# Wo of the last head loaded, bounded and scaled at other slots, and values stored as whole rows

## The reference, cut to what is computed

```
xn = layernorm(x)
q = xn @ Wq;  k, v = split(xn @ Wkv)
scores = q k^T / sqrt(32) + slope[head] * (s - t), only s <= t
attn = softmax(scores);  o = attn v
attention = concat(o) @ Wo + bo
gate = xn @ Wg^T;  up = xn @ Wu^T        # codes looked up and scaled by blocks of 32
ffn = (gelu_tanh(gate) * up) @ Wd^T
out = x + attention + ffn
```

## Time and profile before

| | |
|---|---|
| median of 3 runs | 1640.24 us (1639.86 to 1642.94) |
| the profiled execution | 1641.02 us |
| its span in the trace | 1639.2 us |
| busy: TensorE | 1429.3 us, 87% |
| busy: VectorE | 1297.4 us, 79% |
| busy: GpSimd | 1000.8 us, 61% |
| busy: ScalarE | 975.9 us, 60% |
| DMA share of the 16 engines, q1 | 80.8% |

### The profile page before, as it was taken

The page is one execution under the profiler, slowest core; times in us unless marked ns, Lnnn a source line. Parts: engine busy times, 40 slices in busy tenths (PEclk is TensorE's granted clock), DMA queues, the critical chain, the costliest instruction groups (busy, mean ns, idle before and its releaser), DMA issues.

```text
span 1639.2 us, 28993 instructions
## 1 busy us (share of the span) xinstructions
PE 1429.3 (87%) x9281; PEld 684.1 (42%) x9281; DVE 1297.4 (79%) x2639; ACT 975.9 (60%) x2124; POOL 1000.8 (61%) x670
## 2 busy tenths in 40 slices
PE   5978998999889989889989989899888999897598
PEld 4743443444334434444434434344433444343243
DVE  8858787888868788888868788888868788875466
ACT  3347666666656666665666666666656666664330
POOL 3226676666656677666656666777656766774341
PEclk9979999999999999999999999999999999998799
DMA  7878969788897888798889879886998988887665
GB/s 219 231 176 175 171 119 170 149 161 154 160 163 144 160 155 165 145 152 149 166 158 153 157 151 160 147 174 136 173 154 154 153 158 153 147 152 133 120 155 198
DMA packets 784799, 260.97 MB, mean 159 GB/s; under 512 B 734512, under 2 KB 755896, under 8 KB 784392
## 3 DMA queue, kind: packets, MB, share of 16 engines
q1 hardware_dynamic: 780328, 253.48, 80.8%
q10 hardware_dynamic: 4320, 5.64, 1.0%
HBM read 52.30 MB, written 21.89 MB: 45 GB/s over the span
## 4 chain that ended last, share of the span: by engine, by line
DVE 30%; PE 18%; issue 14%; ACT 10%; DMA 10%; POOL 6%; SPq 4%; ACTq 0%; DVEq 0%; POOLq 0%
DMA pt<-pair 8%; PE up_ps L1348 5%; ACT p L1475 5%; POOL pair L1734 5%; DVE mxp L1588 4%; DVE acc L1545 4%; PE gate_ps L1348 4%; PE s_ps L1370 3%; DVE dec L369 3%; DVE wf L382 3%; DVE prod L1569 2%; PE down_ps L1326 2%; ACT gl L1456 2%; DVE s_ps L1590 2%; DVE dec L373 2%
## 5 line engine op out<-in xcount | busy, mean ns | idle before, releaser
L1734 POOL TENSOR_TENSOR pair<-p,pair 128x1024 f16<-128x1024 f32 (+7 forms) x384 | 615.2, 1610 | 347.3 <-ACT pair L1485 344.9
L1475 ACT ACTIVATE p<-s_ps,shift 128x512 f32<-128x512 f32 (+3 forms) x640 | 393.2, 619 | 222.6 <-DVE shift L1609 220.9
L1370 PE MATMUL s_ps<-kst,qst 128*128 128x512 f32 (+3 forms) x640 | 344.7, 540 | 115.2 <-ACT p L1475 106.9
L1485 ACT ACTIVATE pair<-p 128x1024 f16<-128x1024 f32 (+7 forms) x384 | 308.3, 808 | 100.4 <-DMA pt<-pair 97.3
L1588 DVE TENSOR_REDUCE mxp<-s_ps 128x1 f32<-128x512 f32 x384 | 260.2, 683 | 103.5 <-PE s_ps L1370 101.5
L1742 POOL TENSOR_TENSOR il<-prod,ih 128x512 f16<-128x512 f32 x128 | 156.2, 1220 | 149.7 <-DVE ih L1577 149.7
L1370 PEld LDWEIGHTS s_ps<-kst,qst 128*128 128x128 f32 x640 | 123.2, 193 | 233.6 <-ACT p L1475 157.9
L1326 PE MATMUL down_ps<-wh,ih 128*128 128x512 f16 x506 | 195.9, 387 | 28.2 <-DVE acc L1545 28.2
L1326 PE MATMUL down_ps<-wh,il 128*128 128x512 f16 x506 | 193.0, 381 | 16.0 <-POOL il L1742 16.0
L1348 PE MATMUL up_ps<-xh,wh 128*128 128x512 f16 x512 | 200.2, 391 | 0.0
L1348 PE MATMUL gate_ps<-xh,wh 128*128 128x512 f16 x512 | 197.6, 386 | 0.6 <-DVE gl L1561 0.6
(11 more groups left out here) (249 smaller groups left out, 2064.6 us busy)
## 6 DMA issues: line engine op xcount, KB each, us to landing
o<-oraw SPq DMA_DIRECT2D x256, 64.0 KB, 2.0
qst<-q_parts SPq DMA_DIRECT2D x192, 64.0 KB
q_parts<-o SPq DMA_DIRECT2D x24, 256.0 KB, 3.4
pt<-pair SPq DMA_TRANSPOSE x384, 4.3
raw<-L_ffn_gate_W_packed_dram SPq DMA_DIRECT2D x16, 256.0 KB, 3.1
raw<-n_L_ffn_up_W_packed_dram SPq DMA_DIRECT2D x16, 256.0 KB, 3.0
raw<-L_ffn_down_W_packed_dram SPq DMA_DIRECT2D x32, 128.0 KB, 2.6
o<-l_recips SPq DMA_DIRECT2D x64, 64.0 KB, 2.1
```

The source lines that it names most:

```text
L1370: nc.tensor.matmul(s_ring[n % len(s_ring)][:, 0:cols], qst[:, c % 2, i4 * P:(i4 + 1) * P], kst[:, m * CH:m * CH + cols], start=True, stop= ...
L1475: nc.scalar.activation(p32[p % PR][:, at:at + cols], s_ring[n % len(s_ring)][:, 0:cols], ACT.Exp, bias=shift[t % len(shift)][:, 0:1], accu ...
L1485: nc.scalar.activation(pair[n % PH][:, 0:cols], p32[n % PR][:, 0:cols], ACT.Copy).then_inc(phi_done, 1)
L1734: nc.gpsimd.tensor_tensor(pair[n % PH][:, cols:2 * cols], p32[n % PR][:, 0:cols], pair[n % PH][:, 0:cols], ALU.subtract).then_inc(plo_done, 1)
```

## The change

Six slot numbers move, one step is cut in two, and the layout of the stored values changes.

- `LOAD_EARLY_AT` 12 becomes 1; `WO_MAX_AT` (17, 18, 19, 20) becomes (14, 16, 17, 19).
- `spread_tops` is divided: `store_tops` stores the maxima at slot 21; `spread_tops`, which waits for the store, reads them back and issues `load_full(sp, 1)`, is at slot 28 instead of 27.
- `WO_SCALE_AT` 29 becomes 37, `WO_HI_AT` (31, 32, 33, 34) becomes (38, 40, 42, 43), `wo_low` follows one slot behind each; `LOAD_X_AT` 41 becomes 46.
- `vt` and `v_s` hold two fields instead of four; the fills and their semaphore go; `load_v` is one DMA of 256 KB, 2 KB in a row per partition on both sides.

```diff
-LOAD_EARLY_AT, LOAD_FULL_AT, SPREAD_TOPS_AT, LOAD_X_AT = 12, 25, 27, 41
+LOAD_EARLY_AT, LOAD_FULL_AT, STORE_TOPS_AT, SPREAD_TOPS_AT, LOAD_X_AT = 1, 25, 21, 28, 46
-WO_MAX_AT, WO_SCALE_AT, WO_HI_AT = (17, 18, 19, 20), 29, (31, 32, 33, 34)
+WO_MAX_AT, WO_SCALE_AT, WO_HI_AT = (14, 16, 17, 19), 37, (38, 40, 42, 43)
-    v_s = nc.dram_tensor("v_parts", [KVH, P, NT, 4 * HD], F16, kind="Internal").ap()
+    v_s = nc.dram_tensor("v_parts", [KVH, P, NT, 2 * HD], F16, kind="Internal").ap()
-    vt = wh[1][:, 0:2].rearrange("p m a n -> p (m a n)").rearrange("p (j g a d) -> p j g a d", j=TPC, g=KVH, a=4)
+    vt = wh[1][:, 0].rearrange("p a n -> p (a n)").rearrange("p (j g a d) -> p j g a d", j=TPC, g=KVH, a=2)
-                nc.gpsimd.memset(vt[:, :, :, 1, :], 1.0).then_inc(vt_filled, 1)
-                nc.gpsimd.memset(vt[:, :, :, 3, :], 0.0).then_inc(vt_filled, 1)
-                    for part in range(2):
-                        sp.dma_start(vst[:, :, part * HD:(part + 1) * HD],
-                                     v_s[i // REP, :, :, 2 * part * HD:(2 * part + 1) * HD]).then_inc(v_in, 16)
+                    sp.dma_start(vst[:], v_s[i // REP]).then_inc(v_in, 16)
+                            if s == STORE_TOPS_AT:
+                                store_tops()
-                def spread_tops():
+                def store_tops():
                     sp.wait_ge(wtop_done, 1)
                     sp.dma_start(w_s.rearrange("(p o) -> p o", o=1), wtop).then_inc(wtop_out, 16)
+
+                def spread_tops():
                     sp.wait_ge(wtop_out, 16)
-                            pe.wait_ge(v_in, (h // REP + 1) * 32)
+                            pe.wait_ge(v_in, (h // REP + 1) * 16)
```

More of the change, by code:

```diff
@@ L539, in preamble @@
         vscale_done = sem("vscale_done")
-        vt_filled = sem("vt_filled")
         os_turned = sem("os_turned")
@@ L572, in store_v @@
                     sp.wait_ge(v_lo, c + 1)
-                    if c == 0:
-                        sp.wait_ge(vt_filled, 2)
                     store_values(sp, c)
@@ L921, in values_lo @@
                     nc.vector.scalar_tensor_tensor(
-                        vt[:, :, :, 2, :].rearrange("p j g d -> p (j g) d"), vps[:].rearrange("p (n d) -> p n d", d=HD),
+                        vt[:, :, :, 1, :].rearrange("p j g d -> p (j g) d"), vps[:].rearrange("p (n d) -> p n d", d=HD),
                         vscale[:, 0:1], vt[:, :, :, 0, :].rearrange("p j g d -> p (j g) d"), ALU.mult, ALU.subtract
```

## The result

The changed kernel took **1612.92 us** (median of 4 runs, 1609.45 to 1614.90), the kernel before 1640.05 us beside it (4 runs): ratio 0.9837, 95% interval 0.9822 to 0.9852. Forecast were 1606 us, with a range of 1594 to 1618. So it is faster by 27 us where 35 were forecast. The profiled execution took 1613.71 us, its span is 1611.9 us.

What follows compares the result with a forecast made beforehand. TensorE was taken to set the pace in the running stream, with losses waiting for Wo, the stored maxima and the values. Gains of 19 + 2 + 12 + 2 = 35 us off 1641.02 gave 1606 us, range 1594 to 1618.

Steps and rivals of the forecast that it cites:

- Term 1: Last head, wait for the stored maxima: storing at slot 21, reading at 28, using at 37 gains 19 us (14 to 21).
- rival (a): Last head: transposes held behind the store at slot 21, 5 us of idle and 2 of clock, 1613 us; chance 0.15.
- transposes over 8 us behind the store: Store at slot 21: transposes taking over 8 us behind it would show the prediction wrong.
- 1.8 us given back at the end: Before the last values product: moved weight splittings let the last transpose start earlier, 1.8 of TensorE's 2.75 us saved.
- Term 2: Last head, wait for Wo: its load moved from slot 12 to slot 1 gains 2 us (-4 to +14).
- rival (b): Slot 1 has room: transposes pass the Wo load and values wait nowhere, gain 14, 1594 us; chance 0.08.
- (c): Hold at slot 1 felt twice, at tiles 5 and 7 and again at the scores: -4, 1612 us; chance 0.15.
- Term 3: Three values loads at group boundaries: one DMA of whole rows, shorter waits and no clock fall, 12 us (4 to 16).
- 4 us as a sign of being wrong: Values loads: one landing after 4 us or more would show the prediction wrong.
- Term 4: First values load, ahead of the loop: a saved second issue and a lighter queue gain 2 us (0 to 5).
- Rival (e): Single values DMA falls on one engine at 25 GB/s: 14 us slower, 1654 us; chance 0.03.
- Rival (d): Values load gains only its issue time, 1.0 us each, and the clock still falls: 1614 us; chance 0.13.

Runs made afterwards that it cites:

- low_moved: The changed kernel with the splitting of Wo at slots 39, 42, 43, 44 instead of 38, 40, 42, 43; 1611.86 us, ratio 0.9850 to the kernel before.
- load12: The changed kernel with Wo's load back at slot 12 and the maxima at slots 17 to 20; 1613.84 us, ratio 0.9849 to the kernel before.
- after_again: The changed kernel run once more without an edit; 1614.62 us, ratio 0.9863 to the kernel before.
- store_act: The changed kernel with the store of the maxima issued from ScalarE's queue at slot 21 instead of SyncE's; 1615.81 us, ratio 0.9869 to the kernel before.
- best: The changed kernel with Wo in eight DMAs over all engines, maxima stored in four 128-byte pieces, Wo splitting at slots 39, 42, 43, 44; 1603.88 us.
- v_only: The changed kernel with all Wo slots of the kernel before, so the values part alone; 1628.52 us, ratio 0.9929 to the kernel before.

## Why the prediction came out as it did

Direction and range held; 8 us of the 35 did not come, 5 in the last head and 3 before it. Between the first and the second profile 27.3 us went.

**Term 1 (19 forecast, 14.6 measured) carries most of it.** The pause went nearly as said: the step from 36 to 42 shrank by 16.6, where 15.6 for the pause and 2.6 for the clock, less the 1 us charged, make 17.2. The steps next to it lost 2.7 (30 to 36) and 0.6 (42 to 48), and the last product runs 1.2 us shorter, at full clock. Two entries of the sum were mis-sized. "I charge 1 us, with 4 as bound" for what now stands in the running stream left out the store: rival (a) came true, in mechanism and in landing (10.28 us where it said 11.6), at 2.7 us in its own step and 3.0 by the kernels with the other store, where it was priced at 7. The prediction had named transposes over 8 us behind the store as a sign of being wrong, and gave this rival 0.15. And of the 1.8 us given back at the end some 0.7 came (1.2 less 0.6). The pause of 2.75 us before the last values product did go, but the splittings beside GpSimd's work took 1.51 and 2.60 us, not 0.7, and TensorE waited 3.04 us. The prediction asked for VectorE's free time there, but not for GpSimd's; `low_moved` gave 3.4 to 3.8 us back in that step.

**Term 2 (2 forecast, about 0 measured).** The step that the prediction worked out is there: 9.25 us of TensorE idle for 9.5, ScalarE standing beside it, the share at 0.26, the transpose 10.86 us after its issue. 12 to 24 lost 11.3 us (9.5 + 1.8 + 1.0 forecast), 24 to 30 gained 12.7, net 1.4 by the two traces; `load12`, which undoes this term alone, puts it at about 0 over these steps (38.23 us against 38.43 and 38.12) and at -2 over the whole last head. Within the bounds of -4 and 14; rival (b) fell, and (c) did not come as TensorE's wait, since tile 7 cost none.

**Term 3 (12 forecast, 8 to 9 measured).** The distance of a decoding step from the same a head later answers to the earlier trace rows:

```profile
1128.14 2.46 DVE wf L382
...
1219.41 2.47 DVE wf L382
...
1307.36 2.47 DVE wf L382
```

91.27 us with a load, where it was 95.26 and the prediction said 91; 87.95 without. Over heads 4, 8 and 12 that is 9.4 us; over all profiles (eleven with the new load, three with the old) 276.7 against 285.1, so 8.3. The waits fell by 5.2, not 6.6: the landings are 3.0, 3.1 and 4.0 us, the last as slow as the old ones at their best, and 5.2 to 5.3 us in `after_again`, `store_act` and `best`. The prediction had named 4 us as a sign of being wrong; at head 12 it came true in those three. Of the 5.4 us for the clock some 3 to 4 came (8.3 to 9.4 less 5.2), since the second wait, 1.99 us, still brought the clock to 0.50 (the last of the windows above). Behind the other two, of 1.31 and 1.29 us, it stayed up, as the prediction claimed:

```profile
482.50:484.00 1.50, 1.50 (x13) 0.73 (x14) 1.43 (x6) 1.14 (x3) 0.91 (x1) 1.00 0.83 192
1204.00:1206.00 2.00, 2.00 (x21) 0.82 (x18) 1.15 (x3) 1.68 (x3) 1.42 (x2) 1.00 0.69 136
```

The length of the wait alone doesn't decide it: in `after_again` one of 2.68 us at head 12 was followed by a clock of 1.00.

**Term 4 (2 forecast, about 1 measured).** SyncE's queue answers to the earlier trace rows:

```profile
114.70 0.34 SPq L1165 DMA_DIRECT2D vst<-v_parts  x1
115.10 3.82 SPq L1196 DMA_TRANSPOSE pt<-pair  x3
```

1.7 us of issue are saved. From this issue to the first decoding step of the loop it is 113.2 us, before 114.7; as means of eleven and three profiles 113.3 and 114.3, with single ones from 111.6 to 114.9, so the 1 us is only just seen.

Rival (e) fell: 256 KB as one DMA land in 3.1 us. Rival (d) had a third of its case, the clock.

## What to carry to other kernels

A store or load is priced by its pieces and by the engines on which it falls, and whoever queues behind it pays: look for a DMA share far under 1 while others wait, and for pieces of a few bytes. Moving such a DMA to another slot moves the pause; changing its shape (32 rows outermost instead of 4, pieces of 128 bytes instead of 4) removed 6 and 3 us here. Where VectorE work is moved, ask what GpSimd does there, and put it behind the instruction that others wait for; then look at the tail, where part of the gain may be waited away again.

## What the runs showed that was not expected

- An all-reduce over the partitions on GpSimd that counts 0.38 us took the engine out for 13.4 us.
- A store of 512 bytes in 4-byte pieces took 8.0 to 11.6 us to land in every place, and held transposes of another queue, one of which had begun its issue 0.5 us ahead of it.
- Profiles with the same instructions up to there reached the first values load between 112.61 and 118.17 us, and the mark of 12 in the last head between 1462.19 and 1473.38. Two profiles can't show 2 us ahead of the last head.
- With unchanged code the last head was 4.9 us shorter in `v_only` than before (its two pauses were 11.27 and 13.56 us, not 12.20 and 15.58). Whether the lighter values load did that or chance is open; the profiled execution was the fastest of its six.
